# Weights of a matrix pass read with a step of two: item parts stored in pairs of chunks

## What is computed

```python
h = item_feat @ W_item.T + b_item             # 10000 x 128
b = layernorm(x) @ W_user.T + b_user
x = x + relu(adj @ h + b)                     # adj is 10000 x 10000, float32
# then an LSTM over the 10000 rows (4 gates, width 128), logits, a running sum of gated rows
x = x + lstm_block(layernorm(x))
```

## Time and profile before

| | |
|---|---|
| median of 3 runs | 1426.8 us |
| the profiled execution | 1429.61 us, of which the span of the profile is 1427.8 us |
| stage one | to about 1126 us |
| stage two | about 302 us |
| TensorE busy | 1401.8 us (98%) |
| VectorE busy | 1273.0 us (89%) |
| ScalarE busy | 1056.4 us (74%) |
| DMA | 443 MB, mean 310 GB/s over the span |

### The profile page before, as it was taken

The page is one execution under the profiler, slowest core; times in us unless marked ns, Lnnn a source line. Parts: engine busy times, 40 slices in busy tenths (PEclk is TensorE's granted clock), DMA queues, the critical chain, the costliest instruction groups (busy, mean ns, idle before and its releaser), DMA issues.

```text
span 1427.8 us, 26195 instructions
## 1 busy us (share of the span) xinstructions
PE 1401.8 (98%) x7438; PEld 1210.5 (85%) x7438; DVE 1273.0 (89%) x2102; ACT 1056.4 (74%) x1449; POOL 213.4 (15%) x189
## 2 busy tenths in 40 slices
PE   8999999999999999999999999999999999999995
PEld 7888888888888888888888888888888899999995
DVE  7999999999999999999999999999999766676667
ACT  5677787777877877877877877877877676556663
POOL 0000000001001001001001001001000132036776
PEclk9999999999999999999999999999999999999998
DMA  9999999999999999999999999999999303000003
GB/s 373 344 336 382 399 387 392 394 385 383 405 385 395 391 387 397 392 382 402 384 387 402 391 377 405 387 380 402 388 388 382 133 1 144 0 2 0 0 0 145
DMA packets 143466, 442.96 MB, mean 310 GB/s; under 512 B 23944, under 2 KB 43337, under 8 KB 143307
## 3 DMA queue, kind: packets, MB, share of 16 engines
q1 hardware_dynamic: 126048, 426.43, 76.7%
q10 hardware_dynamic: 17387, 16.14, 4.0%
HBM read 432.15 MB, written 10.36 MB: 310 GB/s over the span
## 4 chain that ended last, share of the span: by engine, by line
PE 93%; DVE 5%; ACT 0%; issue 0%; DMA 0%; POOL 0%; ACTq 0%; DVEq 0%
PE psG L882 24%; PE psG L883 24%; PE psG L884 24%; PE psZ L980 10%; PE psZ L966 3%; PE psZ L968 3%; PE psZ L970 3%; DVE a_lo L1201 2%; PE psZ L986 1%; PE psT L857 1%; PE psI L930 1%; DVE item_lo L1234 1%; DVE u L1516 1%; DVE u L1215 0%; PE psG L875 0%
## 5 line engine op out<-in xcount | busy, mean ns | idle before, releaser
L665 ACT ACTIVATE a_hi<-raw 128x1000 fp32r<-128x1000 f32 (+1 forms) x800 | 819.5, 1030 | 241.9 <-PE psG L884 212.7
L1201 DVE TENSOR_TENSOR a_lo<-raw,a_hi 128x1000 fp32r<-128x1000 f32 (+1 forms) x800 | 897.8, 1171 | 22.9 <-ACT a_hi L665 19.9
L882 PE MATMUL psG<-a_hi,item_hi 128*128 128x500 f32 x1560 | 611.3, 392 | 2.3 <-DVE a_lo L1201 1.4
L883 PE MATMUL psG<-a_lo,item_hi 128*128 128x500 f32 x1560 | 606.0, 388 | 0.0
L884 PE MATMUL psG<-a_hi,item_lo 128*128 128x500 f32 x1560 | 604.6, 388 | 0.0
L882 PEld LDWEIGHTS psG<-a_hi,item_hi 128*128 128x128 f32 x1560 | 293.5, 188 | 65.5 <-DVE a_lo L1201 3.5
L884 PEld LDWEIGHTS psG<-a_hi,item_lo 128*128 128x128 f32 x1560 | 293.1, 188 | 59.5
L883 PEld LDWEIGHTS psG<-a_lo,item_hi 128*128 128x128 f32 x1560 | 293.7, 188 | 55.5
L980 PE MATMUL psZ<-hist,wh 128*128 (+1 forms) x1264 | 167.1, 275 | 2.9 <-DVE hist L1354 2.2
L980 PEld LDWEIGHTS psZ<-hist,wh 128*128 128x128 f32 x1264 | 154.0, 191 | 3.8 <-issue 2.4
L466 POOL TENSOR_TENSOR row_terms<-var,minus_half 125x4 f32<-125x4 f32 x20 | 37.6, 1878 | 677.9 <-DVE var L1152 677.9
(11 more groups left out here) (186 smaller groups left out, 857.1 us busy)
## 6 DMA issues: line engine op xcount, KB each, us to landing
raw<-in_adj_main SPq DMA_DIRECT2D x760, 500.0 KB, 6.6
raw<-in_adj_main SPq DMA_DIRECT2D x40, 250.0 KB, 4.7
sq<-rstd_copy ACTq DMA_DIRECT2D x20, 250.0 KB, 7.0
u<-x_copy SPq DMA_DIRECT2D x1, 5000.0 KB, 14.4
x_copy<-x_rows SPq DMA_DIRECT2D x19, 250.0 KB, 7.2
sq<-rows_copy ACTq DMA_DIRECT2D x19, 250.0 KB, 5.3
un_bb<-rows_copy ACTq DMA_DIRECT2D x19, 250.0 KB, 7.6
u<-in_itemT SPq DMA_DIRECT2D x9, 512.0 KB, 8.0
```

The costliest lines, as they stand in the source:

```text
L665: nc.scalar.activation(a_hi[:, s % CUT, 0:n], raw[:, r % RAW, at:at + n], ACT.Copy)\
L882: pe.matmul(bank, w_hi, hi, start=(c == 0), stop=False)
L883: pe.matmul(bank, w_hi, lo, start=False, stop=False)
L1201: last = dve.tensor_tensor(a_lo[:, s % CUT, 0:m], raw[:, r % RAW, at:at + m], a_hi[:, s % CUT, 0:m].bitcast(f32), ALU.subtract)
```

## The change

The two tiles `item_hi` and `item_lo` keep their size, but two chunks now share 256 columns: the even chunk has columns 0, 2, 4, ..., the odd one 1, 3, 5, ... So the weights of each of L882 to L884 are 128 columns with a step of two elements. The last, short chunk stays as it was. To have the values in that order, `item_quad` writes each product with a step of two into `psI`, and the bias tile `bi` holds each value twice (256 columns, copied from PSUM by one instruction); `u`, `item_hi` and `item_lo` are then written as before, in one run of elements.

To make room, `inv_rows` and `item_tail` move into a part of `x1_rows` that is free then, and five small tiles move between the large ones. By that the tiles of the rings start at other addresses within a partition: `item_lo` 110016 instead of 110208, `raw` 150464 instead of 150656, `a_hi` 182560 instead of 182656, `a_lo` 198560 instead of 198656; `item_hi` stays at 69440. Stage two's tiles stay where they were, but for `wi`, 512 bytes lower.

No engine gets another instruction or another order: the list of each engine has the same operations on the same shapes, but for the copy of `bi`, which is 256 wide instead of 128.

```diff
-        bi = sb("bi", [P, HID])
+        bi = sb("bi", [P, 2 * HID])
...
         item_hi = sb("item_hi", [P, (CH + 1) * HID], f32r, first)
-        item_tail = sb("item_tail", [P, STACKED], f32, first)
+        moments = sb("moments", [SW, SUB, 6], f32, first)
+        mean_sum = sb("mean_sum", [SW, SUB], f32, first)
         item_lo = sb("item_lo", [P, (CH + 1) * HID], f32r, first)
         raw = sb("raw", [P, RAW, MAXC * BW], f32, first)
+        mean_gap = sb("mean_gap", [SW, SUB], f32, first)
+        gap_sq = sb("gap_sq", [SW, SUB], f32, first)
+        spread = sb("spread", [SW, SUB], f32, first)
...
+        def item_cols(c):
+
+            return slice(c // 2 * PAIR + c % 2, (c // 2 + 1) * PAIR, 2) if c < CH else slice(c * HID, (c + 1) * HID)
...
-                            w_hi = item_hi[:, c * HID:(c + 1) * HID]
-                            w_lo = item_lo[:, c * HID:(c + 1) * HID]
+                            w_hi = item_hi[:, item_cols(c)]
+                            w_lo = item_lo[:, item_cols(c)]
...
+            def quad_cols(c):
+                k = c % 4
+                return slice(k // 2 * PAIR + k % 2, (k // 2 + 1) * PAIR, 2) if c < CH else slice(k * HID, (k + 1) * HID)
...
-                    last = pe.matmul(psI[0:rows, q % 2, (c % 4) * HID:(c % 4 + 1) * HID], columns, wi[:, :],
+                    last = pe.matmul(psI[0:rows, q % 2, :][:, quad_cols(c)], columns, wi[:, :],
                                      start=True, stop=True)
...
-                    dve.tensor_tensor(dst.rearrange("p (c h) -> p c h", h=HID),
-                                      psI[:, q % 2, 0:n * HID].rearrange("p (c h) -> p c h", h=HID),
-                                      bi[:, :].unsqueeze(1).to_broadcast([P, n, HID]), ALU.add)\
+                    dve.tensor_tensor(dst.rearrange("p (c h) -> p c h", h=PAIR),
+                                      psI[:, q % 2, 0:n * HID].rearrange("p (c h) -> p c h", h=PAIR),
+                                      bi[:, :].unsqueeze(1).to_broadcast([P, n // 2, PAIR]), ALU.add)\
...
-            dve.tensor_copy(bi[:, :], psW[:, 0:HID]).then_inc(bi_ready, 1)
+            dve.tensor_copy(bi[:, :].rearrange("p (h e) -> p h e", e=2),
+                            psW[:, 0:HID].unsqueeze(2).to_broadcast([P, HID, 2])).then_inc(bi_ready, 1)
```

More of the change, by code:

```diff
@@ L35 @@
 STACKED = STACK[-1] + TAIL
+PAIR = 2 * HID
+assert CH % 2 == 0
 PIECES = 20
@@ L120, in program @@
         minus_half = sb("minus_half", [P, 1])
-        inv_rows = sb("inv_rows", [2, P])
         wi = sb("wi", [P, HID])
@@ L143, in program @@
         total = sb("total", [P, 1])
-        wd, dfd = wi, bi
+        wd, dfd = wi, bi[:, 0:HID]
         first = ExitStack()
         item_hi = sb("item_hi", [P, (CH + 1) * HID], f32r, first)
-        item_tail = sb("item_tail", [P, STACKED], f32, first)
+        moments = sb("moments", [SW, SUB, 6], f32, first)
+        mean_sum = sb("mean_sum", [SW, SUB], f32, first)
         item_lo = sb("item_lo", [P, (CH + 1) * HID], f32r, first)
         raw = sb("raw", [P, RAW, MAXC * BW], f32, first)
+        mean_gap = sb("mean_gap", [SW, SUB], f32, first)
+        gap_sq = sb("gap_sq", [SW, SUB], f32, first)
+        spread = sb("spread", [SW, SUB], f32, first)
         a_hi = sb("a_hi", [P, CUT, HALF * BW], f32r, first)
@@ L158, in program @@
         bi_row = x1_rows[0:1, HID:2 * HID]
+        item_tail = x1_rows[:, 2 * HID:2 * HID + STACKED]
+        inv_rows = x1_rows[0:2, 3 * HID:4 * HID]
         normed = x1_rows
@@ L166, in program @@
         v = un_bb[:, 0:BW]
[L167 to L171, removed]
         var = sb("var", [SW, SUB], f32, first)
@@ L874, in body @@
                             if c == CH:
-                                last = pe.matmul(bank, item_hi[0:STACKED, c * HID:(c + 1) * HID],
+                                last = pe.matmul(bank, item_hi[0:STACKED, item_cols(c)],
                                                  a_hi[0:STACKED, s % CUT, i * BW:(i + 1) * BW], start=False, stop=True)
@@ L1222, in item_sum_part @@
                 dve.wait_ge(prep, 1)
[L1223 to L1226, removed]
+                pair, single = slice(0, PAIR), slice(PAIR, PAIR + HID)
+                for part, a, b in ((pair, 0, P), *((single, a, a + TAIL) for a in STACK)):
+                    dve.tensor_tensor(sq[a:b, part], psI[a:b, q % 2, part],
+                                      bi[a:b, :] if part is pair else bi[a:b, 0:PAIR:2], ALU.add)\
                         .then_inc(item_sum if a == STACK[-1] else prep, 1)
```

## The result

The changed kernel took 1432.7 us (median of 8 runs, 1430.96 to 1433.55) against 1426.9 us of the kernel before (8 runs, 1426.64 to 1429.94): ratio 1.0032, 95% interval 1.0021 to 1.0043. It is slower by about a third of a per cent, just over what this kernel's measurement can tell. The forecast was 1406 us, its own range 1385 to 1421 us. The wide range of 1377 to 1435 us holds the result only because it took in the rivals.

What follows compares the result with a forecast made beforehand. TensorE was taken to bound the kernel, VectorE and DMA within 5%. 1427.8 - 20.9 (blocks 1 to 19) + 0.1 = 1407.0 us of span, 1406 us against the median; range 1377 to 1435 us, the forecast's own 1385 to 1421.

Steps and rivals of the forecast that it cites:

- What bounds the kernel: Blocks of 54.6 us: TensorE never pauses, 0.2257 us a pass; VectorE busy 52.0 us, DMA share 1.01.
- The reading of the surplus: Each TensorE pass carries 17.4 ns beyond its columns, from moving-column reads and next weights' loads getting in each other's way.
- the price of 0.214 us: Pass with step-two weights, priced from plain float32 passes of equal stream speed; TensorE's own block 51.8 us, 2.8 less.
- The bounds: Price of a pass with step-two weights: best 0.2083 us, no surplus; worst 0.243 us, surplus doubled.
- Rival A: Passes: more places touched, more conflicts; doubled surplus +83 us, 1510 us, a fifth of it 1443 us; chance 0.18.
- Rival B: Passes: surplus is the float32r pass's own, so a step changes nothing, 1427 us; chance 0.14.
- What is late next: Blocks 1 to 19: with faster passes the DMA sets 53.5 us a block instead of 54.6, saving 20.9 us.
- Rivals C and D: C: DMA gives no more, 1423 to 1427 us, chance 0.03; D: DMA gives all asked, 1377 us, chance 0.08.
- The first block and PSUM: First block: faster passes bring 0, VectorE being busy; item products written to PSUM with a step of two cost 0.
- rival E: First block: strided PSUM write costs its full double, 17.7 us more, 1424 us; chance 0.05.
- The copy of `bi`: Path of the start: copy 256 wide instead of 128, taken as +0.1 us.

Runs made afterwards that it cites:

- m1_passes: No kernel computation, only a copy of x and groups of 16 equal TensorE passes: 225.3 ns a pass with step one, 227.2 step two, 234.9 step four.
- e3_13_passes_less: Kernel before, leaving out the item_hi against a_lo pass for every sixth chunk, 13 of 238 passes a block: 1402.3 us, ratio 0.982.
- e4_39_passes_less: Kernel before, leaving out the item_hi against a_lo pass for every second chunk, 39 of 238 passes a block: 1402.2 us, ratio 0.9815.
- e6_slots_best: Kernel before, weights without a step, slices 2048 bytes apart, a_hi and a_lo starting 192 bytes above the weights modulo 256: 1412.9 us, ratio 0.9899.
- e2_addresses_only: Kernel before, weights without a step, but the tiles at the changed kernel's addresses: 1427.3 us, ratio 0.9997.
- e5_step_four: Kernel before, but blocks 1 to 19 read the weights of chunks 0 to 75 with a step of four: 1476.2 us, ratio 1.0334.
- e7_slots_worst: e6_slots_best with other spacers, a_hi 64 and a_lo 96 bytes above the weights modulo 256: 1443.3 us, ratio 1.011 against the kernel before.

## Why the prediction was wrong

*What bounds the kernel* was right: TensorE without a pause, 225.7 ns a pass, three resources within 5%.

*The reading of the surplus* was right in one half. It arises with TensorE alone at work and depends on the addresses of its two reads, which fits the pattern that repeats between blocks. That these reads get into each other's way stays an argument. The other half failed, and it is **the step of the prediction that went wrong: "when the two streams walk through memory at equal speed they settle side by side", and with it the price of 0.214 us taken from the plain float32 passes**. A pass with a step of two took 226.6 ns in the kernel and 227.2 alone. Plain float32 and bfloat16 both take 210.6 ns. The nearest rows by relative speed were not the nearest rows: they differed in data format as well, and in the bytes that the moving stream reads in a given time. Which of the two makes the 210.6 ns no run tells.

*The bounds* had been put at 0.2083 and 0.243 us, and the truth lay inside, 0.9 ns above the price before. Rival A's mechanism, more places touched, comes closest: the load went from 188 to 195 ns and to 316 with a step of four. The Trainium skill, "Advanced Engine Details and Errata" (Memory Cachelines), says that SBUF lines hold 16 bytes and that at least two accesses to a line are needed for full speed. The trace agrees in the order: a load with two weights in a line took 7 ns more than one with four, and a load with one in a line 128 ns more, though part of the 316 ns is waiting, since 256 such loads fit into 60.14 us. The price in time per pass is another thing and was far smaller than I had put for A. For a step of two it was 1.9 ns over the 16 starts of `m1_passes`, 0.1 ns over the 256 pairs and 0.9 ns in the kernel; for a step of four it was nearly 10.

*Rival B's page*: I had quoted "TensorE: Matmul & The Clock Gate" (Part 2, step 1) of the Trainium skill for loads that take nothing from a running matmul. In bfloat16 the trace agrees, 210.6 ns; in float32r a pass pays 12 to 23 ns by the starts of the two operands, and the number of weight columns does not change the mean. So no run shows that it is the load that takes this time; what is refuted is B's own claim that a step changes nothing.

*What is late next*: 53.5 us had been predicted for a block whose passes are fast enough, and 1406 us. `e3_13_passes_less` and `e4_39_passes_less` gave 53.2 and 53.4 us and 1402 us. The size of this term was right, with some luck, since it was read off the landings of two blocks; that it is the DMA alone, and not VectorE together with it, is not shown. `e6_slots_best`, 14 us faster than the kernel before, shows that two thirds of the gain were there to be had, only not by this change. Rivals C and D, as they were put, are refuted by the same runs.

*The first block and PSUM.* The item products written with a step of two: 140 records between 10 and 87 us,

```profile
L940 PE MATMUL psI<-wi,u 128*128 128x128 f32 x140 | 18.6, 275 | 0.0
```

against 19.5 us for as many before. Their starts say the same: 111 or 112 ns apart in most cases in either kernel. So there is no cost, as taken, and rival E falls. The Trainium skill, "PSUM — Partial Sum Buffer" (Specifications (TRN2)), has it otherwise; the trace does not agree for these float32 passes, which write a column only every second cycle (250 columns in 210.6 ns), and a full-speed write with a step was not tried. The copy of `bi` took 0.42 instead of 0.29 us, +0.13 where 0.1 was taken; the two rows that the 0.10 came from give 0.13 themselves, (0.69 - 0.29) / 3. The first block ended at 84.7 us in this profile and at 86.9 in that of before; but `e2_addresses_only`, with contiguous weights, ended it at 84.7 us too and `e5_step_four`, whose first block is that of before, at 87.0, so this says nothing of the change.

What stays open: what in TensorE makes the charge of 12 to 23 ns in float32r, and why no placement with a step of two, whose loads last 195 ns, got to 220. Shown is that it changes with the distance of the two starts, with a period of 256 bytes, and that it is there without other traffic, with operands of zeros, at widths from 256 to 512 columns and, in the mean, alike for 32 to 128 weight columns. The distance alone does not fix it: the same one gave 220 and 229 ns in different surroundings.

## What to carry to other kernels

Where TensorE is the bound with float32r passes, place the moving slices at one fixed distance from the weights modulo 256 bytes (a slice length of 2048 instead of 2000 bytes does it here, with weights 512 bytes apart) and search that distance with bare passes in one run. Use the kernel's own sequence of passes for it, since one repeated pass had its good distances elsewhere, and check the winner in the kernel: here it was worth 1%, and the best placement held its 220 ns in the full kernel, the worst did not hold its 231. Keep the weights contiguous: no step of two reached 220 ns. And before pricing a change by the nearest rows, ask in how many respects they differ: cutting the work by the hoped-for amount tests the second half of an argument at once, a small program of bare passes the first.

## What the runs showed that I had not expected

- A float32r pass of 500 columns costs 220 to 231 ns by placement alone, at the full clock, against 210.6 in bfloat16.
- The loads of 32 weight columns last 108 ns instead of 188, and the passes beside them are no faster.
- With the same distance, and even with the same starts, bare passes settle at one pitch or another: 223.4 or 226.6 ns with both starts at 0, 220 or 229 at 64 bytes.
- The layout before had 225.7 ns, by chance 1 ns under the mean of the placements tried. Moving tiles alone was worth 0.07 us a block in `e2_addresses_only`, and 30 us between `e6_slots_best` and `e7_slots_worst`.
- With a step of four, or with 192 columns, the loads of weights have no idle time left.
